# Eight routed experts: when ScalarE rounds the next expert's first matrix, and how GpSimd subtracts it

## The reference

```python
buf = zeros((E, cap, D)).at[e, pos_c].set(xt * keep, mode='drop')
h = gelu(einsum('ecd,edf->ecf', buf, w1) + b1[:, None, :])
y = einsum('ecf,efd->ecd', h, w2) + b2[:, None, :]
a = einsum('ecr,erd->ecd', gelu(einsum('ecd,edr->ecr', buf, wd)), wu)
y = y + a
```

## Time and profile before

| | us |
|---|---|
| median of 3 runs | 844.95 |
| lowest, highest of them | 844.93, 2498.66 |
| the profiled execution | 844.81 |
| span of its profile | 843.0 |
| busy in the span: TensorE matmul | 827.7 |
| VectorE | 627.4 |
| ScalarE | 475.1 |
| GpSimd | 471.1 |

### The profile page before, as it was taken

How to read it: one execution, slowest core, us unless ns; L and a number is a source line. 1 busy time by engine, 2 the same in 40 slices (tenths; PEclk the granted TensorE clock), 3 DMA queues, 4 the chain that set the end, 5 groups by cost and what they waited for, 6 DMA issues and landing times.

```text
span 843.0 us, 15621 instructions
## 1 busy us (share of the span) xinstructions
PE 827.7 (98%) x5436; PEld 709.8 (84%) x5436; DVE 627.4 (74%) x1273; ACT 475.1 (56%) x948; POOL 471.1 (56%) x327
## 2 busy tenths in 40 slices
PE   8999999999999999999999999999999999999998
PEld 7888888888867799999998878888889988886688
DVE  6899999999997655665666869587677785446767
ACT  3666766666674565655553375743353426367743
POOL 6676767676684845575767011009939216718820
PEclk9999999999999999999999999999999999999999
DMA  8101010100006376456213150011111010030001
GB/s 341 38 20 37 19 37 19 37 19 29 9 1 226 129 265 196 161 171 207 88 39 94 51 200 14 1 50 43 46 37 38 13 63 1 2 150 3 2 2 51
DMA packets 23343, 62.18 MB, mean 74 GB/s; under 512 B 3136, under 2 KB 13632, under 8 KB 20224
## 3 DMA queue, kind: packets, MB, share of 16 engines
q1 hardware_dynamic: 21760, 57.35, 19.9%
q0 software_dynamic: 1536, 4.20, 1.5%
HBM read 50.00 MB, written 8.39 MB: 69 GB/s over the span
## 4 chain that ended last, share of the span: by engine, by line
PE 80%; DVE 9%; POOL 4%; ACT 3%; issue 2%; DMA 1%; SPq 0%; DVEq 0%; POOLq 0%
PE banks L102 23%; PE banks L104 23%; PE banks L103 23%; PE banks L1382 3%; POOL slots L767 2%; POOL arenaC L866 1%; PE banks L1368 1%; DVE stats L1457 1%; DVE x L1452 1%; PE banks L1014 1%; PE banks L958 1%; PE banks L957 1%; PE banks L879 1%; POOL rstd L648 1%; PE banks L1001 1%
## 5 line engine op out<-in xcount | busy, mean ns | idle before, releaser
L2145 ACT ACTIVATE banks<-banks,small 128x512 f32<-128x512 f32 x128 | 84.9, 663 | 70.8 <-DVE small L1517 70.8
L1517 DVE TENSOR_REDUCE small<-banks 128x1 f32<-128x512 f32 x128 | 86.8, 678 | 4.4 <-PE banks L104 4.4
L104 PE MATMUL banks<-arenaC_rounded,arenaD_rounded 128*128 128x512 f32 (+1 forms) x256 | 89.3, 349 | 0.0
L102 PE MATMUL banks<-xnT_rounded,arenaD_rounded 128*128 128x512 f32 x224 | 87.7, 392 | 0.7 <-POOL arenaC_rounded L732 0.4
L103 PE MATMUL banks<-s_tok_rounded,arenaD_rounded 128*128 128x512 f32 x224 | 87.1, 389 | 0.0
L104 PE MATMUL banks<-xnT_rounded,arenaD_rounded 128*128 128x512 f32 x192 | 74.8, 390 | 0.0
L104 PE MATMUL banks<-xnT_rounded,arenaC_rounded 128*128 128x512 f32 x192 | 74.7, 389 | 0.0
L102 PE MATMUL banks<-arenaC_rounded 128*128 128x512 f32 (+1 forms) x192 | 70.9, 369 | 1.2 <-DVE arenaC L1532 0.6
L1532 DVE SCALAR_TENSOR_TENSOR arenaC<-banks,small,arenaC 128x512 f32<-128x512 f32 x96 | 71.2, 742 | 0.0
L103 PE MATMUL banks<-arenaD_rounded,arenaC_rounded 128*128 128x512 f32 (+1 forms) x192 | 67.9, 354 | 0.0
L718 POOL TENSOR_TENSOR arenaD_rounded<-arenaC,ones 128x512 fp32r<-128x512 f32 x30 | 31.3, 1042 | 47.5 <-DVE arenaC L1532 46.4
(11 more groups left out here) (444 smaller groups left out, 2689.8 us busy)
## 6 DMA issues: line engine op xcount, KB each, us to landing
arenaD<-in_wexp SPq DMA_DIRECT2D x8, 1060.0 KB, 6.1
arenaD<-in_wexp SPq DMA_DIRECT2D x8, 1024.0 KB
arenaC<-in_wqkv SPq DMA_DIRECT2D x16, 384.0 KB, 3.0
arenaD<-in_wexp SPq DMA_DIRECT2D x8, 512.0 KB, 3.6
slots<-arenaB SPq DMA_DIRECT2D x1, 2560.0 KB, 10.0
arenaB<-in_sw SPq DMA_DIRECT2D x1, 2084.0 KB, 7.5
arenaC<-in_wo SPq DMA_DIRECT2D x1, 2048.0 KB, 14.4
arenaC<-slots SPq DMA_DIRECT2D x8, 256.0 KB, 3.2
```

What stands on the lines that cost most here:

```text
L102: pe.matmul(o, r(lhs[0]), r(rhs[0]), start=start, stop=False)
L104: return pe.matmul(o, r(lhs[1]), r(rhs[0]), start=False, stop=stop)
L1517: dve.tensor_reduce(negmax[:, n % 4:n % 4 + 1], bank[3 + n % 4][:, :], AX.X, ALU.max, negate=True).then_inc(max_done, 1)
L2145: act.activation(prob[r], prob[r], ACT.Exp, bias=negmax[:, r:r + 1], accum_out=rowsum[:, r:r + 1]).then_inc(exp_done, 1)
```

## The change

Two edits. On ScalarE only three blocks of the next w1 are rounded between the gelus, behind gelus 2, 3 and 4. The fourth block and wd are rounded behind the slots, in the loop that goes on with w2; the wait for `w2exp0_in` stands ahead of that loop. On GpSimd the subtraction of w1 is two instructions of 1024 columns: the first waits for two roundings and counts nothing, the second waits for four and adds the one to `w_split` that the whole added before. The first expert (`late`) is left as it was.

```diff
                 if not late:
-                    part_of(4, w[:, 0:W_D], hi[:, 0:W_D])
+                    pool.wait_ge(w_rounded, 10 * e + 2)
+                    pool.tensor_tensor(r(w[:, 0:1024]), w[:, 0:1024], rounded(hi[:, 0:1024]), ALU.subtract)
+                    part_of(4, w[:, 1024:W_D], hi[:, 1024:W_D])
                     down(5)
...
-                    if 2 <= n < 7:
+                    if 2 <= n < 5:
                         if n == 2:
                             act.wait_ge(sw_in if last else w1exp_in[1 - q], 48 if last else 16 * turn + 16)
                         round_weights(...)
                 if not last:
                     round_rows(e + 1, 1 - q)
                     act.wait_ge(w2exp0_in[1 - q], 48 * turn + 48)
-                for n in range(5, 9):
+                for n in range(3, 9):
                     round_weights(...)
```

## The result

| | before | changed |
|---|---|---|
| median, us | 844.97 | 853.3 |
| lowest run | 844.93 | 852.81 |
| profiled span | 843.0 | 851.4 |

The ratio of changed to before is 1.0099, with a 95% interval from 1.0087 to 1.0111: 1.0% slower, 8.3 us. One of the four runs of the kernel before took 2498.66 us; it moves neither the median nor the ratio, and nothing here explains it.

What follows compares the result with a forecast made beforehand. TensorE was taken to bound the kernel, its matmuls busy for 827.7 of 843.0 us. Six waits summing to 8.20 us, with nothing gained elsewhere, took 844.81 to 853.0 us, 1.0% slower, range 848.5 to 858.5.

Steps and rivals of the forecast that it cites:

- Part 1: ScalarE's gelus 5, 6 and 7: two roundings leave from between them; worth at most 1.4 us, taken as nothing.
- Part 2: ScalarE's bias wait: 3.86 us of rounding, subtraction and hand-overs now follow the landing, delaying TensorE 8.20 us over six experts.
- The six waits: TensorE ahead of the hidden products of experts 2 to 7: waits of 0.82 to 2.06 us, 8.20 us in sum.
- No expert catches up: Routed experts: if TensorE begins later, the bias's issue and landing move with it, so the waits add up.
- The copy behind the wait: ScalarE's copy of the result: some 0.9 us later, but covered, as TensorE needs it only behind the second hidden block.
- The signs: Changed profile: six weight-load waits for GpSimd, 8 us; stretches of 17.6 to 18.8 us; bias landing 13.7 to 15.0 us in.
- Expert 1 and the shared one free: Ahead of these two ScalarE doesn't wait for a load; the chain would end 2.6 us before TensorE's need.
- Part 3: GpSimd's w1 subtraction in two halves: worth nothing alone on TensorE, but without it each wait grows 2.2 us.
- The rival with the bias in time: ScalarE's bias wait: the bias lands early enough, not slower, 846.0 us less at most 1.4; chance 0.08.
- point of decision: Bias landing: no wait is left if it comes 3.86 us ahead of TensorE's need, at 362.36 for expert 4.
- The late landing: Bias load's queue: it lands 1.5 us later on average, mean wait 2.8 us, giving 862 us; chance 0.04.
- the freed gelus: ScalarE's gelus: roundings did hold TensorE back, so seven gaps of 0.20 us go, giving 843.4 us; chance 0.02.

Runs made afterwards that it cites:

- e1_ahead: Changed kernel with w1's fourth block and wd still rounded behind the slots, but ahead of the `w2exp0_in` wait: 844.34 us, ratio 1.0003.
- e9_quarter: Changed kernel with GpSimd's w1 subtraction split 1536 + 512 columns instead of 1024 + 1024, the first piece waiting for three roundings: 847.39 us, ratio 1.0037.
- e3_halves: Kernel before with only GpSimd's w1 subtraction split in two halves, ScalarE's order as before: 844.39 us, ratio 1.0002.
- e5_wd: Changed kernel with w1's fourth block rounded ahead of the `w2exp0_in` wait and wd alone behind it: 844.15 us, ratio 0.9999.

## Why the prediction was right

- **The bound.** TensorE sets the pace, and nothing that the change does on ScalarE or GpSimd is worth anything to it. Right: with the wait taken away and the rest of the change kept, e1_ahead is at the time of before.
- **Part 1, the roundings that leave the gelus: nothing.** Right within 0.1% (e1_ahead, which has only three of them between the gelus too, 1.0003).
- **Part 2, the chain of 3.86 us.** Measured 3.90 ahead of expert 4. The hand-over from GpSimd to TensorE, which the trace of before didn't show, is 370.59 - (369.73 + 0.74) = 0.12 us; I had taken 0.08.
- **The six waits.** Forecast and measured, experts 2 to 7: 2.06 and 1.57; 1.00 and 1.15; 1.17 and 1.56; 1.09 and 1.36; 2.06 and 1.86; 0.82 and 0.53. The sums are 8.20 and 8.03. The single values are off by up to 0.5 us either way, since I took each landing from the trace of before, and the landings vary; the sum is good because the errors fell on both sides. In e9_quarter they mostly fell on one side (the two late issues of the bias load alone brought 1.4 us), and the same reckoning was 1.7 us short. The good agreement of the total, 853.0 against 853.3 us, is partly luck.
- **No expert catches up, and the waits add.** Right: 8.06 us from expert 1 to expert 7.
- **The copy behind the wait, covered.** Right: it began 3.22 us behind the landing (369.91 - 366.69) in place of 2.40, so 0.8 us later, where I had 0.9, and TensorE didn't wait for it.
- **The signs.** Two were set too narrow. The stretches of experts 2 to 7 (each up to the beginning named) are 18.36, 17.91, 18.32, 18.13, 18.62 and 17.29 us, and the last is under the 17.6 that I gave. The bias lands 13.42 to 14.72 us after the hidden products begin, and the 13.42, ahead of expert 7, is under the 13.7 whose breach I had called a sign of being wrong. The mean is 14.2 us, where the trace of before has 14.3, so the mechanism stands, and the limits left no room for a landing that varies. GpSimd's halves came as forecast: the first began 5.66 us after the hidden products (357.93 - 352.27), the second 0.69 us after the landing.
- **Expert 1 and the shared one free.** Right: no wait of TensorE is there.
- **Part 3, the halves.** Right: nothing alone (e3_halves), and 13.7 us of wait saved over the six experts behind the wait, 1.8 to 2.8 us each, 2.3 on the mean. That "each of the six waits would be 2.2 us longer" without them was short of the truth in time, since longer waits also cost clock: 23.0 us (876.3 - 853.3), or 23.9 by the two losses, not 13.3.
- **The rival with the bias in time.** It didn't occur. Its point of decision did show up in e5_wd, whose chain is 2.6 us shorter (1.34 in place of 3.90) and costs nothing. One of its grounds was misread: the store of twice the size is L561 (256 KB), and the one just ahead of the bias is L562, of 64 KB. The sum doesn't use it.
- **The page's fixed cost.** The Trainium skill ("DMA: Bandwidth & Descriptors", "Anatomy of one DMA") gave 2.3 us for this load, as an estimate from its figures for the software path. The changed trace doesn't agree either: ScalarE is released at 366.69, 4.0 us after SyncE's issue at 362.65.
- **The late landing, the freed gelus.** Neither occurred.
- **What can be told from no change.** The prediction says about 2%. The intervals of these runs are 0.1 to 0.25% to either side, so the 1.0% is clear, and so are the experiments' 0% and 0.4%.

## What to carry to other kernels

When work moves behind an existing wait, read what that wait ends on, and how long before the next need it ends; a wait that costs nothing is no longer free once something urgent stands behind it. The price is the chain from the wait's end to the need less the time between them, for each turn of the loop, and here it came out right to 0.1 us in the chain and to 1 us in the landing. A semaphore that counts loads with different needs makes the earliest user wait for the last load, so give the late one its own.

## What the runs showed of the hardware

Waits of TensorE of up to 1.86 us left its clock at full speed (1.00 in every stretch of the changed kernel). With waits of 2.8 to 4.1 us the granted clock was 0.50 to 0.62 over the 4 us behind five of six, and 1.00 behind one of 3.36 us. Six waits of 21.7 us together so cost some 10 us more in slow matmuls, and with 2.84 us of needless products ahead of each wait the clock stayed at 1.00 and the kernel was 8.5 us faster. The Trainium skill ("TensorE: Matmul & The Clock Gate", "Part 1: The HAM clock gate") says that TensorE's clock falls to half when the array has been idle, and comes back with work; the two runs agree, and they show that whether it falls isn't told by the length of a single wait alone, since 2.76 us was followed by a fall and 3.36 us wasn't.

The landing of one load of 128 KB, issued in the same order in every kernel, came 3.1 to 4.8 us after its issue. The time goes by the place more than by the kernel: in all eight kernels whose ScalarE waits for it, the landing ahead of expert 6 came 4.3 to 4.7 us after the issue and the one ahead of expert 7 3.1 to 3.4. In the stretches in which TensorE held the full clock and had no wait inside, the issue came 10.3 to 10.4 us after the hidden products began where the store's issue ahead of it (L562) took 0.51 or 0.52 us, and 11.0 to 11.6 where that took 1.1 to 1.6.
